# A paged-attention layer stack on one core: the first sample's loads spread over a tile, output weights in GpSimd's queue, one value block read by VectorE

## The chip, the cores and the metric

The kernel runs on one core of a Trainium2 chip. A core has five engines that run side by side: TensorE (matrix products, transposes), VectorE, ScalarE, GpSimd, and SyncE (SP), which here only issues DMAs. They meet through semaphores. The 16 DMA engines of the core serve SP's queue and GpSimd's queue. The metric is device time in microseconds of one execution, the median of several runs.

## The reference

64 samples of 32 tokens with 512 features go through four residual steps. The last is by far the heaviest:

```python
q, k, v = x @ Wq, x @ Wk, x @ Wv                 # 32 query heads, 8 key/value heads of 128
q, k = rope(rmsnorm(q)), rope(rmsnorm(k))
kc, vc = k_cache[block_table], v_cache[block_table]      # 16 pages of 32 positions per sample
scores = q @ concat([kc, k]) * SCALE             # masked to cache_seqlens
o = softmax(scores) @ concat([vc, v])
x = x + o @ Wo
```

Everything is float32 in the reference; the kernel splits numbers into a high and a low 16-bit part and multiplies the parts.

## The kernel before

The program has three blocks, one after another, with all engines meeting between them (a wait for `PEq L884` in the trace is the meeting at the end of the projections): `mixing` (the first three steps), `projections` and `attention`.

`projections` runs over NT = 16 tiles of 128 rows (four samples each). A tile is BLK = 12 blocks of 512 columns: 8 of queries, 2 of keys, 2 of values. TensorE makes a block in 12 matrix products; for queries and keys ScalarE sums squares, VectorE multiplies by the rotation tables, GpSimd adds, TensorE transposes the heads, ScalarE and VectorE keep the high and low halves, and SP stores them (`store_heads`). Each value block is read from PSUM twice by ScalarE (lines 1318, 1319), once in float32 and once in bfloat16; GpSimd forms the rest (`rest`), ScalarE the middle part (`middle`), GpSimd the lowest (`rest_low`), one tile later. Beside this the cache and output weights are split in chunks: SP loads chunk m + 2 and stores chunk m - 1 (`chunks`), ScalarE and VectorE split it. Once a tile ScalarE takes a square root (line 1293). SP's queue also carries the two DMA transposes of the next tile's input (`turn_x`, line 1088).

All SP work is one hand-written order: `body(t, p)` goes over the 12 blocks `n` and issues what is due. At the last block of tile EARLY = 12, `first_sample` (line 1096) waits for what it needs and calls `load_sample`, `load_fresh` and `load_row_scales`: everything of sample 0 that attention will need, 30 DMAs. Sample 1 is sent in pieces in the last tile (`second_sample`, line 1113).

`attention` has units of one sample and one key head: U = 32 units in a group of four samples, 512 in all. Per unit TensorE makes scores, transposes the probabilities of two units ago, and weighs values of three units ago; from the second group on it also projects one head of the group before (`project`). VectorE adds the mask and finds the maximum, ScalarE takes exponentials, VectorE normalises, GpSimd splits the probabilities of the new tokens (`new_tokens`, line 1735), which TensorE transposes (`turn_new`). There are two buffers for keys: SP fetches sample b when the scores and exponentials of sample b - 2 are done (`load`, line 1667): new keys, query, four small loads of scales (line 145), 16 pages (line 169), and four loads of fresh values (line 186). GpSimd gathers the values (line 1730). The output weights, 8 chunks of 1 MB, are issued by SP too: `WO_BEHIND` says behind which sample, four at the start and one behind each of samples 2 to 5, and `load_wo` waits for the chunk before (lines 1684 to 1688):

```python
if c:
    sp.wait_ge(wo_in[(c - 1) % 2], 16 * ((c - 1) // 2 + 1))
heads = (c * WOH, (c + 1) * WOH)
sp.dma_start(wo_of(*heads), wo_d[:, heads[0]:heads[1], :, :]).then_inc(wo_in[c % 2], 16)
```

TensorE waits for a chunk every fourth head of the first projected group (line 1833).

## Time and profile before

| | us |
|---|---|
| median of 3 runs (2137.56 to 2142.57) | 2138.86 |
| profiled execution | 2142.95 |
| its span | 2141.2 |
| TensorE busy | 2067.9 (97%) |
| VectorE busy | 1679.1 (78%) |
| ScalarE busy | 1476.0 (69%) |
| GpSimd busy | 1104.0 (52%) |
| DMA | 514.10 MB, 240 GB/s in the mean |

`mixing` ends and `projections` begins before 197 us, attention begins at 755.6 us. In the rows below, a timeline row gives the start and the duration in us, the engine, the line of the kernel, the operation with its output and inputs, and in brackets how long the engine had been idle before it and whom it waited for. PE is TensorE, PEld its weight loads, DVE VectorE, ACT ScalarE, POOL GpSimd, SPq the queue of SP. A window row gives for each engine the busy us and the instructions in a stretch, then the granted clock of TensorE as a share of full speed, the busy share of the DMA engines, and GB/s.

### The profile page before, as it was taken

The numbers are of one execution on the slowest core, as the hardware profiler recorded it, in microseconds if no ns is written. First come the engines' busy times: TensorE is split into PE (matmuls) and PEld (weight loads), VectorE is DVE, ScalarE is ACT, GpSimd is POOL, SyncE is SP. The second block draws the span as 40 slices with busy tenths as digits, with TensorE's granted clock in tenths as the row PEclk, the third lists the DMA queues.
The fourth block names the chain that finished last, engine by engine and source line by source line (L and its number), as shares of the span: only waits on it lengthen the run. The fifth ranks groups of instructions, "written<-read, shape, count | busy, mean of one in ns | idle before, by whom it ended". The sixth has DMA issues, their size and how long they took to land.

```text
span 2141.2 us, 55701 instructions
## 1 busy us (share of the span) xinstructions
PE 2067.9 (97%) x17214; PEld 1349.8 (63%) x17214; DVE 1679.1 (78%) x4282; ACT 1476.0 (69%) x4204; POOL 1104.0 (52%) x1855
## 2 busy tenths in 40 slices
PE   7989999999998978999999999999999999999999
PEld 3544555555554556777777777777777777777775
DVE  6897888888886676777777777777777777777774
ACT  2457777777776666777777777777777777777774
POOL 4456656565665634545454445455454545454542
PEclk9999999999999989999999999999999999999999
DMA  7755778776777778888888878788888888888881
GB/s 277 267 215 169 248 226 249 225 243 201 233 239 221 245 249 280 260 249 251 247 259 246 253 244 262 238 254 251 248 250 250 252 254 245 251 255 247 250 242 57
DMA packets 417577, 514.10 MB, mean 240 GB/s; under 512 B 67299, under 2 KB 313955, under 8 KB 416260
## 3 DMA queue, kind: packets, MB, share of 16 engines
q1 hardware_dynamic: 379828, 375.65, 57.5%
q0 software_dynamic: 37456, 134.89, 19.6%
q8 instruction: 142, 2.33, 0.4%
q14 instruction: 151, 1.24, 0.2%
HBM read 413.91 MB, written 92.54 MB: 237 GB/s over the span
## 4 chain that ended last, share of the span: by engine, by line
PE 60%; SPq 1%; DMA 1%; issue 1%; DVE 1%; ACT 0%; DVEq 0%; POOL 0%; POOLq 0%; ACTq 0%
PE att_y L1839 15%; PE att_scores L1789 15%; PE att_tr L1798 11%; PE att_o L1825 5%; PE att_o L1826 5%; PE att_o L1827 5%; PE att_tr_new L1804 1%; PE att_o L1828 1%; PE att_scores L1790 1%; DMA w<-wo_parts 1%; SPq L169 1%; DMA room<-k_parts 1%; SPq L145 0%; DVE att_prob L1942 0%; DVE att_tpl L1966 0%
## 5 line engine op out<-in xcount | busy, mean ns | idle before, releaser
L1942 DVE CUSTOM_DVE_ANT_0 att_prob<-att_scores,att_mask 128x544 f32<-128x544 f32 x512 | 370.9, 724 | 292.3 <-PE att_scores L1790 239.3
L1868 ACT ACTIVATE att_tph<-att_tr 128x512 f16<-128x512 f32 x512 | 305.9, 597 | 329.6 <-PE att_tr L1798 321.9
L1872 ACT ACTIVATE att_prob<-att_prob,att_col,rscale 128x544 f32<-128x544 f32 x512 | 430.7, 841 | 55.1 <-DVE att_col L1948 17.4
L1740 POOL CAST att_parts<-att_norm 128x96 f16<-128x96 f32 x512 | 135.1, 264 | 569.9 <-issue 556.8
L1966 DVE TENSOR_TENSOR att_tpl<-att_tr,att_tph 128x512 f16<-128x512 f32 x512 | 350.3, 684 | 1.1 <-ACT att_tph L1868 0.9
L1798 PE MATMUL att_tr<-ident,att_norm 128*128 128x128 f32 x2048 | 327.4, 283 | 0.0
L1354 POOL TENSOR_TENSOR proj_rn<-proj_ra,proj_rb 128x512 f32<-128x512 f32 x128 | 188.6, 1474 | 203.9 <-DVE proj_rb L1482 202.7
L1825 PE MATMUL att_o<-att_tph,w 128*128 128x128 f16 x1536 | 284.4, 219 | 2.8 <-ACT att_of L1868 2.4
L1826 PE MATMUL att_o<-att_tpl,w 128*128 128x128 f16 x1536 | 284.4, 219 | 0.0
L1827 PE MATMUL att_o<-att_tph,w 128*128 128x128 f16 x1536 | 284.4, 219 | 0.0
L1798 PEld LDWEIGHTS att_tr<-ident,att_norm 128*128 128x128 f32 x2048 | 216.5, 142 | 61.9 <-issue 1.4
L1959 DVE TENSOR_SCALAR att_norm<-att_prob,att_col 128x544 f32<-128x544 f32 x512 | 254.2, 497 | 1.0 <-issue 1.0
L1249 ACT ACTIVATE proj_square<-proj_blk 128x128 bf16<-128x128 f32 x640 | 168.4, 283 | 115.5 <-PE proj_blk L1209 115.5
L1789 PE MATMUL att_scores<-room 128*128 128x512 f16 x768 | 225.2, 383 | 15.0 <-DMA room<-k_parts 5.3
L1789 PE MATMUL att_scores<-w 128*128 128x512 f16 x768 | 220.6, 377 | 1.8 <-DMA w<-k_parts 1.4
L1730 POOL DMA_INDIRECT w<-v_parts,att_idx x186 | 184.1, 990 | 48.0 <-POOL att_idx L1728 24.6
L1825 PEld LDWEIGHTS att_o<-att_tph,w 128*128 128x128 f16 x1536 | 150.6, 98 | 30.3 <-issue 2.2
L1478 DVE TENSOR_TENSOR proj_ra<-proj_blk,proj_ta 128x512 f32<-128x512 f32 x160 | 110.0, 688 | 71.2 <-ACT proj_square L1249 69.4
L1839 PE MATMUL att_y<-w,att_ot 128*128 128x512 f16 x576 | 155.6, 379 | 0.0
L1839 PE MATMUL att_y<-w,ot 128*128 128x512 f16 x576 | 151.9, 379 | 0.0
L1827 PEld LDWEIGHTS att_o<-att_tph,w 128*128 128x128 f16 x1536 | 150.6, 98 | 0.0
L1826 PEld LDWEIGHTS att_o<-att_tpl,w 128*128 128x128 f16 x1536 | 150.6, 98 | 0.0
(234 smaller groups left out, 5423.7 us busy)
## 6 DMA issues: line engine op xcount, KB each, us to landing
room<-k_parts SPq DMA_DIRECT2D x512, 128.0 KB
w<-k_parts SPq DMA_DIRECT2D x512, 128.0 KB
q_parts<-ot SPq DMA_DIRECT2D x128, 256.0 KB, 3.8
v_new_parts<-ot SPq DMA_DIRECT2D x64, 256.0 KB
room<-q_parts SPq DMA_DIRECT2D x32, 512.0 KB
w<-q_parts SPq DMA_DIRECT2D x32, 512.0 KB
w<-in_w_t SPq DMA_DIRECT2D x12, 1024.0 KB, 7.7
room<-in_k_t SPq DMA_DIRECT2D x8, 1024.0 KB, 7.3
```

The source lines that it names most:

```text
L1354: g.tensor_tensor(out[:, :], ra[n % 2][:, :], rb[n % 2][:, :], ALU.add).then_inc(sum_done, 1)
L1789: mm(old, a, k, start=start, stop=stop)
L1798: last = nc.tensor.transpose(tr[q][:, c * P:(c + 1) * P], old[:, c * P:(c + 1) * P], ident[:, :])
L1825: mm(out, vh, th, start=(c == 0), stop=False)
L1826: mm(out, vh, tl, start=False, stop=False)
L1827: mm(out, vl, th, start=False, stop=False)
L1839: last = mm(y_ps[:, :], ot[p][:, a, h, :], wo_of(h, h + 1)[:, 0, w, :], start=(h == 0 and start), stop=(h == HQ - 1 and stop))
L1868: copy = lambda out, in_, **kw: nc.scalar.activation(out, in_, ACT.Copy, **kw)
L1872: nc.scalar.activation(prob[q][:, :], prob[q][:, :], ACT.Exp, bias=col[q][:, 1:2], scale=row_scale(i), accum_out=col[q][:, 2:3]).then_inc( ...
L1942: v.tensor_tensor_reduce(out=prob[q][:, :], in0=sc[q], in1=mask[bi % 2][:, at:at + LK], scale=1.0, scalar=-3.0e38, op0=ALU.add, op1=ALU.ma ...
L1959: v.tensor_scalar(out=norm[q][:, :], in0=prob[q][:, :], scalar1=col[q][:, 3:4], scalar2=TOP, op0=ALU.mult, op1=ALU.mult).then_inc(norm_don ...
L1966: v.tensor_tensor(tpl[q][:, :], tr[q][:, :], tph[q][:, 0:L], ALU.subtract).then_inc(tl_done, 1)
```

## The change

Four edits. The first sample's loads: at the end of tile 12 only the new keys and the query are issued; in tile 13 `first_rest(n)` issues two pages behind each of blocks 0 to 7, the fresh values behind block 8, and the row scales of samples 0 and 1 behind blocks 9 and 10. The end of the projections: VectorE reads the last value block of the last tile, ScalarE's copies are reordered around the normalising of the keys, and GpSimd finishes value block 0 before block 1. The output weights: GpSimd issues all eight chunks at the start of attention with no wait between them, on one semaphore. And TensorE waits once, ahead of the first projected head, for all eight.

```diff
@@ projections, sync
-                load_sample(nc, sp, 0, 0, 0, keys[0], query[0], rscale[0], page0, k_d, kn_d, q_d, rs_d, early)
-                load_fresh(sp, 0, fresh[0], vn_d, early)
-                load_row_scales(sp, 1, rscale[1], rs_d, early)
+                load_new_keys(sp, 0, keys[0], kn_d, early)
+                load_query(sp, 0, 0, query[0], q_d, early)
+
+            def first_rest(n):
+
+                half, at = divmod(n * 2, NPP // 2)
+                if at == 0 and half < 2:
+                    early_pages[:] = pages_of(nc, 0, half, page0)
+                if half < 2:
+                    for j in (at, at + 1):
+                        load_page(sp, half * (NPP // 2) + j, early_pages[j], keys[0], k_d, early)
+                if n == 8:
+                    load_fresh(sp, 0, fresh[0], vn_d, early)
+                if n in (9, 10):
+                    load_row_scales(sp, n - 9, rscale[n - 9], rs_d, early)
...
+                    if t == EARLY + 1:
+                        first_rest(n)
@@ projections, scalar
                     if t == NT - 1 and n == BLK - 1:
+                        middle(t, 0)
                         for j in range(KB):
                             normalise_keys(t, p, j)
+
+                        break
...
-            for j in range(KB):
-                heads_high(NT - 1, QB + j)
-                middle(NT - 1, j)
+            heads_high(NT - 1, QB)
+            middle(NT - 1, 1)
+            heads_high(NT - 1, QB + 1)
@@ projections, gpsimd
             for j in range(VB):
                 rest(NT - 1, j)
-            for j in range(VB):
                 rest_low(NT - 1, j)
@@ projections, vector
             tiles(dve, body)
+
+            dve.wait_ge(blk_done, NT * BLK)
+            dve.wait_ge(v_read, NT * VB - 1)
+            dve.wait_ge(v_out, (NT - 1) * 4 * 16)
+            dve.wait_ge(vlow, (NT - 1) * VB)
+            j, bank, scale = VB - 1, blk[(BLK - 1) % NB], col[(NT - 1) % 2][:, 6:7]
+            for to in (v32[j][:, :], vp[:, 0, j * D:(j + 1) * D]):
+                last = v.tensor_scalar(out=to, in0=bank[:, :], scalar1=scale, scalar2=None, op0=ALU.mult)
+            last.then_inc(v_read, 1)
@@ attention, sync
-            def load_wo(c):
-                if c:
-                    sp.wait_ge(wo_in[(c - 1) % 2], 16 * ((c - 1) // 2 + 1))
-                heads = (c * WOH, (c + 1) * WOH)
-                sp.dma_start(wo_of(*heads), wo_d[:, heads[0]:heads[1], :, :]).then_inc(wo_in[c % 2], 16)
...
-                    for c in WO_BEHIND.get(t * BT + bi, ()):
-                        load_wo(c)
@@ attention, gpsimd
+            def load_wo(c):
+                heads = (c * WOH, (c + 1) * WOH)
+                g.dma_start(wo_of(*heads), wo_d[:, heads[0]:heads[1], :, :]).then_inc(wo_in, 16)
...
+            for c in range(HQ // WOH):
+                load_wo(c)
             body(0, 0, 0)
@@ attention, tensor
-                if t == 0 and h % WOH == 0:
-                    pe.wait_ge(wo_in[h // WOH % 2], 16 * (h // WOH // 2 + 1))
+                if t == 0 and h == 0:
+                    pe.wait_ge(wo_in, 16 * (HQ // WOH))
```

## Rows read from the trace of the kernel before

**Rows 1.** Windows: us, busy us (instructions) of each engine, clock, DMA share, GB/s.
```profile
594.00:630.00 36.00, 34.88 (x182) 18.40 (x181) 29.87 (x54) 27.39 (x115) 23.43 (x20) 1.00 0.71 214
630.00:666.00 36.00, 28.40 (x134) 14.35 (x132) 20.99 (x38) 19.88 (x88) 15.54 (x11) 0.86 0.81 254
...
795.90:818.40 22.50, 18.55 (x192) 14.13 (x192) 16.71 (x50) 14.92 (x36) 11.29 (x24) 0.92 0.92 295
...
841.80:862.90 21.10, 21.07 (x190) 15.13 (x191) 14.00 (x42) 12.42 (x31) 6.76 (x18) 0.86 0.87 279
...
1005.00:1215.00 210.00, 209.46 (x2146) 151.39 (x2144) 165.50 (x489) 151.34 (x359) 105.33 (x229) 1.00 0.83 251
```

**Rows 2.** Timeline of SP's queue at the end of tile 12: start, duration, what.
```profile
630.24 0.56 SPq L150 DMA_DIRECT2D room<-k_new_parts  x1
...
636.13 9.09 SPq L169 DMA_DIRECT2D room<-k_parts  x16
...
647.14 1.81 SPq L145 DMA_DIRECT2D rscale<-q_row_scales  x4
```

**Rows 3.** Timeline of ScalarE: its square roots of three tiles, and a chunk.
```profile
233.89 0.24 ACT L1293 ACTIVATE proj_ss<-proj_ss 128x40 f32<-128x40 f32 x1 [2.69 <-DVE proj_ss L1442]
...
626.90 0.24 ACT L1293 ACTIVATE proj_ss<-proj_ss 128x40 f32<-128x40 f32 x1 [3.00 <-DVE proj_ss L1442]
...
652.39 0.72 ACT L1228 ACTIVATE proj_chunk_parts<-proj_chunk,up 128x512 f16<-128x512 f32 x1 [10.40 <-DMA proj_chunk<-in_wo_t]
...
674.19 0.24 ACT L1293 ACTIVATE proj_ss<-proj_ss 128x40 f32<-128x40 f32 x1 [3.00 <-DVE proj_ss L1442]
```

**Rows 4.** Timeline of TensorE in the projections, where it had been idle.
```profile
629.41 0.39 PE L1207 MATMUL proj_blk<-w,proj_xt 128*128 128x512 f16 x1 [1.12 <-DMA proj_xt<-xl]
...
654.47 1.09 PE L1186 MATMUL proj_tq<-ident,proj_rn 128*128 128x128 f32 x4 [7.60 <-DVE ot L1488]
```

**Rows 5.** Timeline of TensorE in attention's first 33 units, where it had been idle.
```profile
755.59 0.59 PE L1789 MATMUL att_scores<-room 128*128 128x512 f16 x1 [4.90 <-PEq L884]
...
795.97 0.39 PE L1789 MATMUL att_scores<-room 128*128 128x512 f16 x1 [0.71 <-DMA room<-k_parts]
805.60 0.23 PE L1825 MATMUL att_o<-att_tph,room 128*128 128x128 f16 x1 [1.82 <-DVE att_tpl L1966]
...
818.45 0.39 PE L1789 MATMUL att_scores<-w 128*128 128x512 f16 x1 [1.36 <-DMA w<-k_parts]
...
841.83 0.61 PE L1789 MATMUL att_scores<-room 128*128 128x512 f16 x1 [4.61 <-DMA room<-k_parts]
```

**Rows 6.** Timeline of SP's queue in attention: weights, scales of samples 3 and 6.
```profile
761.66 14.78 SPq L1688 DMA_DIRECT2D w<-wo_parts  x4
...
796.57 6.51 SPq L145 DMA_DIRECT2D rscale<-q_row_scales  x4
...
866.36 2.71 SPq L145 DMA_DIRECT2D rscale<-q_row_scales  x4
```

**Rows 7.** Timeline of ScalarE at the end of the projections: keys normalised.
```profile
747.53 2.44 ACT L1228 ACTIVATE xc<-xc,inv 128x128 f32<-128x128 f32 x8 [0.42 <-DVE inv L1464]
```

**Rows 8.** Timeline of VectorE at the same place.
```profile
747.47 0.69 DVE L1488 TENSOR_TENSOR ot<-proj_tq,ot 128x512 f16<-128x512 f32 x1
```

**Rows 9.** Timeline of GpSimd from the projections' end to attention's first split.
```profile
751.20 1.16 POOL L1359 TENSOR_TENSOR xc<-xc,ot 128x512 f32<-128x512 f32 x1 [3.90 <-ACT ot L1228]
752.31 2.26 POOL L1364 TENSOR_TENSOR ot<-xc,ot 128x512 bf16<-128x512 f32 x2
761.38 0.26 POOL L1740 CAST att_parts<-att_norm 128x96 f16<-128x96 f32 x1 [6.80 <-DVE att_norm L1959]
```

**Rows 10.** DMA queues from 766.6 to 771.3 us: packets, MB, share of 16 engines.
```profile
q1 hardware_dynamic: 144, 1.05, 64.7%
```

**Rows 11.** Instructions of GpSimd's DMA lines: count, min/median/max ns, first and last start.
```profile
L607 POOL DMA_DIRECT2D weights_most<-pow x1: 620/620/620, 70.5 to 70.5; - x1
...
L1730 POOL DMA_INDIRECT w<-v_parts,att_idx x186: 967/973/1086, 793.5 to 2093.2; - x186
```

More of the change, by code:

```diff
@@ L1106, in first_sample @@
                     sp.wait_ge(c_out[i], 16 * SPLIT)
-                load_sample(nc, sp, 0, 0, 0, keys[0], query[0], rscale[0], page0, k_d, kn_d, q_d, rs_d, early)
-                load_fresh(sp, 0, fresh[0], vn_d, early)
-                load_row_scales(sp, 1, rscale[1], rs_d, early)
-            second_pages = []
+                load_new_keys(sp, 0, keys[0], kn_d, early)
[11 more added lines that the diff above has]
+                    load_row_scales(sp, n - 9, rscale[n - 9], rs_d, early)
+            early_pages = []
             def second_sample(n):
@@ L1120, in second_sample @@
                 if at == 0 and half < 2:
-                    second_pages[:] = pages_of(nc, 1, half, page0)
+                    early_pages[:] = pages_of(nc, 1, half, page0)
                 if half < 2:
                     for j in (at, at + 1):
-                        load_page(sp, half * (NPP // 2) + j, second_pages[j], keys[1], k_d, early)
+                        load_page(sp, half * (NPP // 2) + j, early_pages[j], keys[1], k_d, early)
                 if n == 5:
@@ L1599, in attention @@
         y_ps = ctx.enter_context(nc.psum_tensor("att_y", [P, D], F32))
-        wo_in, unmasked = [sem(f"wo_in{i}") for i in range(2)], sem("unmasked")
+        wo_in, unmasked = sem("wo_in"), sem("unmasked")
         kq_in = [sem(f"keys_in{i}") for i in range(2)]
@@ L1631, in quad_views @@
             return src, [ot[p][:, a, heads, bi * S:(bi + 1) * S] for a in range(2)]
-        WO_BEHIND = {0: (0, 1, 2, 3), 2: (4,), 3: (5,), 4: (6,), 5: (7,)}
         def wo_of(first, last):
```

## The prediction

> **What bounds the kernel now.** I read the table of windows first. In the long steady part of attention TensorE is busy 209.46 of 210 us at the full granted clock, and the DMA engines are busy 0.83 of the time [rows 1]: there only TensorE's own work counts, and nothing in this change touches it. So a gain can come only from places where TensorE stands still or runs at a low granted clock. I then listed TensorE's idle times in order of time, and for each looked up the timeline of the engine that it waited for. Three places are near the edit. (1) Tile 13 of the projections: an idle time of 7.60 us [rows 4], and a granted clock of 0.86 in that window instead of 1.00 [rows 1]. (2) The change from projections to attention: 4.90 us idle [rows 5]. (3) The first 33 units of attention (a unit is one sample and one key head): idle times of 0.71, 1.82, 1.36 and 4.61 us [rows 5], with the clock at 0.92 and 0.86 in two windows [rows 1]. After unit 32 TensorE never waits for long, so what is won before it is won at the end.
>
> **Part A, the first sample page by page.** At the end of tile 12 SP issues the whole sample in one go, from 630.24 to 648.95 us [rows 2]: 18.7 us in which it issues nothing else. ScalarE needs the next chunk of raw weights and waits 10.40 us for it [rows 3]; its squares stop, VectorE stops, and TensorE stops for a free head buffer [rows 4]. The price is read best from ScalarE's square root, once a tile: 233.89 to 626.90 us is 11 tiles of 35.73 us; the tile with the stall takes 674.19 - 626.90 = 47.29 us [rows 3]. So 11.6 us are there to be won, idle time and low clock together.
>
> What the edit puts in its place: SP keeps all 30 issues, but in tile 13 has two pages behind each of eight blocks, 2 x 9.09/16 = 1.14 us each [rows 2], and one group of small loads, some 1.8 us, behind each of blocks 8, 9 and 10. A block takes 35.73/12 = 2.98 us. SP's queue also carries chunk loads and stores, head stores and the two transposes of the next tile's input. A chunk load is issued two chunks ahead of its use, three to four blocks or 9 to 12 us, and a quarter of a megabyte lands in less than the 4.9 us that 1 MB takes [rows 6], so a lag of a few us is covered. The transposes have no such cover: TensorE already waited 1.12 us for them at 629.41 [rows 4], and two pages are now ahead of them (1.1 us). The DMA engines are the second limit. A normal tile uses 0.71 x 36 = 25.6 us of them [rows 1]. A sample in steady attention uses 0.83 x 21 = 17.4 us (210 us are ten samples [rows 1]); less its value gathers of 2 MB, at 3.04 us per MB (64.7% of 4.7 us for 1.05 MB [rows 10]), that is 11.3 us. Tile 13 then needs 36.9 us of DMA in 36 us: full. Between ends of 0 and 6.6 us I take 2.0 for both effects, near the wait that the transposes already show. **A = 11.6 - 2.0 = 9.6 us** (5 to 11.6).
>
> **Part B, the last value block on VectorE.** Before, ScalarE normalises the keys from 747.53 to 749.97 [rows 7] and only then reads the second value block; GpSimd has waited 3.90 us for that and runs until 754.57 [rows 9]. TensorE's first score starts 1.02 us later [rows 5]. After: VectorE is free at 748.16 [rows 8], two reads of 0.69 us end at 749.5, GpSimd's first difference (1.16 us) at 750.7. ScalarE has one more copy ahead of the keys, so 747.53 + 0.6 + 2.44 + two copies gives 751.8; GpSimd's last difference (half of 2.26) ends at 752.9, VectorE's last low half about 753.1. VectorE takes the place of GpSimd as the last. **B = 754.57 - 753.1 = 1.5 us** (0.5 to 2.5).
>
> **Part C, output weights in GpSimd's queue.** Before, SP sends four chunks of 1 MB one after another, 14.78 us, and only at 776.44 begins sample 2; one further chunk stands ahead of each of samples 3, 4 and 5 [rows 6]. Behind a chunk the four small scale loads take 6.51 us, without one 2.71 [rows 6]: 3.8 us for each sample. TensorE's waits up to unit 32 are 0.71 + 1.82 + 1.36 + 4.61 = 8.5 us [rows 5]; the low clock costs 0.08 x 22.5 = 1.8 us and 0.14 x 21.1 = 3.0 us [rows 1]. That is 13.3 us at most.
>
> What takes their place: eight chunks without a wait are 8 x 3.04 = 24.3 us of DMA time, and six stores of 0.25 MB ahead of them 4.6 us, so from about 756 they are through at 785. The fetch of sample 2 waits for the exponentials of sample 0. Sixteen units took 795.26 - 755.59 = 39.7 us [rows 5], so eight take 19.8, and it begins near 754.1 + 19.8 = 774. It meets 11 us of chunks and has 11.3 of its own: 796.3. TensorE would be there at 795.26 - 1.5 = 793.8, so it waits 2.5 us (0.7 before), and I charge 1.8 us of low clock as in the window before. Samples 3 and 4 have no chunk ahead; 2 x 3.8 us saved is more than their 1.36 + 4.61 us of waits, and the 1.82 us behind value gathers go with the lighter traffic. TensorE needs the weights from unit 33 on, some 50 us after they have landed; that it now waits for all at once costs nothing.
>
> GpSimd is held while it issues. Its plain DMA took 0.62 us, its gathers 0.97 to 1.09 [rows 11]: 5.0 to 8.7 us for eight. It is first needed 5.8 us into attention [rows 5, 9], and TensorE another 1 us later. I take 0.62 plus 0.3 us between issues, 7.4 us, a loss of 0.7 (0 to 2). **C = 13.3 - 2.5 - 1.8 - 0.7 = 8.3 us** (3 to 13.3).
>
> A rule that speaks against the move: the 186 gathers that GpSimd issued beside VectorE's work are none of them longer than 1.09 us [rows 11]. The Trainium skill, SBUF — State Buffer, section "A bandwidth-pool intuition that's wrong (but worth ruling out)", says that a DMA of GpSimd which takes about 620 ns alone takes about 3100 ns beside a copy on VectorE, since its descriptors wait for a port that the two share. By it eight issues take 24.8 us and the gain falls to about 3 us, an estimate from the page's figure; the trace's gathers don't show it.
>
> **Sum.** 9.6 + 1.5 + 8.3 = 19.4 us. The profiled execution took 2142.95 us (span 2141.2) and would take 2123.5. It is 4.1 us above the median of the three runs, 2138.86; on the median's scale the forecast is **2119.5 us**.
>
> **Rivals.**
> *Tile 13 stays full.* The same issues and 36.9 us of DMA are in one tile; SP's lag eats the chunks' cover and A is about 4. For it: the share of 0.71 before anything is added. Against: SP's regular work in blocks 0 to 6 is one to three DMAs a block, so its lag is small until the transposes. 2138.86 - 4 - 1.5 - 8.3 = 2125. Chance 0.13.
> *The chunks starve sample 2.* Their rows are 8 KB, the pages' 1 KB; if the engines serve queues by turns, pages crawl until 785, and then need some 15 us for issue and landing (776.44 to 795.97 is 19.5 for the whole sample, small loads included). TensorE waits 6.2 us, not 2.5, at a low clock for longer: 2125. Chance 0.14. The Trainium skill, DMA: Bandwidth & Descriptors, "Issuing engines are not separate DMA queues", says that another queue saves issue time only.
> *VectorE delays GpSimd's issues.* Each waits for one VectorE operation, 0.62 + 0.69 us [rows 8, 11]: 10.5 us, 4 us past need, 2124. Chance 0.05. This is the skill's rule as rows price it.
> *The stall is only moved* (the change doesn't do what it says): ScalarE waits in pieces for head stores and chunks, and A is nothing: 2129. Chance 0.05.
> *GpSimd is held until each chunk has landed*, the one that ends slower. A chunk took 14.78/3 = 4.93 us [rows 6], eight 39.4 us; GpSimd's first split of the new tokens comes 33.6 us late, TensorE stands for it, and only the 2.5 us at sample 2 are saved: 19.4 - 31.1 = -11.7, so 2150.5. It decides from a hold of 5.8 + 19.4 + 2.5 = 27.7 us, 3.5 us per issue. Against: the gathers leave GpSimd after 1 us while they are still in flight. Chance 0.05.
>
> **How the numbers follow.** The forecast has 0.58; alone it spans 2115 to 2124. The bounds of A, B and C add up to gains of 8.5 and 27.4 us: 2111.5 to 2130.5, which takes in the first three rivals and the fourth; outside are the last one and sums of several, under 0.2. A measurement here tells about 0.2%, 4.3 us, from no change. The slower case gives 0.05; another 0.05, taken from the forecast and the middle rivals, is for several together, which would end within 4.3 us; faster is 0.90.
>
> **What would show it.** Right, A: the square roots around tile 13 lie about 37.7 us apart, and no chunk wait over 1 us. B: TensorE's first score 1.5 us nearer to its last transpose. C: GpSimd issues eight DMAs in under 9 us, its first split is at most 2 us late, SP's scale loads take under 3 us for samples 3 to 5, TensorE waits 2 to 3 us at unit 16 and hardly at 24 and 32. Wrong: a gap of GpSimd over 10 us, a wait of TensorE for the output weights at unit 33, an interval of tile 13 over 42 us, or new waits in steady attention.

## The result, and the profile after

| | before | after |
|---|---|---|
| median of 7 runs each | 2139.11 us | 2128.31 us |
| lowest and highest run | 2137.56 to 2142.57 | 2125.24 to 2132.66 |
| profiled execution, its span | 2142.95, 2141.2 | 2128.11, 2126.1 |

The ratio is 0.9945, with a 95% interval of 0.9932 to 0.9957: the change wins 11.8 us (9.2 to 14.5), and the medians are 10.8 us apart. The forecast was 2119.5, a gain of 19.4. The direction was right and the time lies in the range of 2111.5 to 2130.5, but outside the 2115 to 2124 to which the forecast itself had given most of its chance: about 0.6 of the forecast gain arrived.

Three landmarks divide both traces into the parts A, B and C of the prediction: ScalarE's square root once a tile, TensorE's first score of attention, and VectorE's first result of a tile of attention. First the roots of tiles 12 to 15 in the changed kernel, from ScalarE's timeline (start, duration, engine, line, operation, in brackets the idle time before it and what ended it), with one head copy that came late:

```profile
628.10 0.24 ACT L1307 ACTIVATE proj_ss<-proj_ss 128x40 f32<-128x40 f32 x1 [3.00 <-DVE proj_ss L1458]
...
663.84 0.24 ACT L1307 ACTIVATE proj_ss<-proj_ss 128x40 f32<-128x40 f32 x1 [1.25 <-DVE proj_ss L1458]
...
667.77 0.60 ACT L1242 ACTIVATE ot<-proj_tq 128x512 f16<-128x512 f32 x1 [1.91 <-DMA q_parts<-ot]
...
703.01 0.24 ACT L1307 ACTIVATE proj_ss<-proj_ss 128x40 f32<-128x40 f32 x1 [3.00 <-DVE proj_ss L1458]
...
737.12 0.24 ACT L1307 ACTIVATE proj_ss<-proj_ss 128x40 f32<-128x40 f32 x1 [1.02 <-DVE proj_ss L1458]
```

Tile 13 takes 663.84 - 628.10 = 35.74 us where it took 47.29 [rows 3]. The whole stall is gone, and tile 13 is a normal tile, not the 37.7 us of the forecast. But tile 14 takes 703.01 - 663.84 = 39.17 us, 3.7 more than the 35.44 that it took in the trace of before (709.63 - 674.19). The roots of tiles 14 and 15 there:

```profile
709.63 0.24 ACT L1293 ACTIVATE proj_ss<-proj_ss 128x40 f32<-128x40 f32 x1 [3.00 <-DVE proj_ss L1442]
743.83 0.24 ACT L1293 ACTIVATE proj_ss<-proj_ss 128x40 f32<-128x40 f32 x1 [1.02 <-DVE proj_ss L1442]
```

The same place in the changed kernel's timelines of TensorE and of SP's queue shows why:

```profile
668.77 0.39 PE L1221 MATMUL proj_blk<-w,xt 128*128 128x512 f16 x1 [2.42 <-DMA xt<-xl]
```
```profile
657.87 2.95 SPq L139 DMA_DIRECT2D v_new_parts<-ot  x4
661.00 1.27 SPq L169 DMA_DIRECT2D room<-k_parts  x2
662.31 0.49 SPq L1069 DMA_DIRECT2D wo_parts<-proj_chunk_parts  x1
662.85 0.43 SPq L1063 DMA_DIRECT2D proj_chunk<-in_wo_t  x1
663.38 0.45 SPq L1046 DMA_DIRECT2D q_parts<-ot  x1
663.94 1.30 SPq L1088 DMA_TRANSPOSE xt<-xh  x1
665.29 1.73 SPq L1088 DMA_TRANSPOSE xt<-xl  x1
```

SP falls behind at the end of tile 13: the transposes are issued only at 663.94 and 665.29, behind two pages, a chunk and stores. TensorE waits 2.42 us for the low half of the next input, where it waited 1.12 at the start of tile 13 in the kernel before [rows 4], and ScalarE 1.91 us for a head store that freed its buffer late. The windows (us, then busy us and instructions of PE, PEld, DVE, ACT and POOL, clock, DMA share, GB/s) show the new traffic of tile 13 and what follows:

```profile
631.00:667.00 36.00, 35.35 (x184) 18.52 (x182) 28.85 (x53) 26.34 (x112) 21.91 (x18) 1.00 0.95 311
667.00:703.00 36.00, 34.23 (x179) 18.29 (x180) 27.88 (x47) 25.09 (x109) 21.87 (x18) 1.00 0.71 212
...
1005.00:1215.00 210.00, 209.63 (x2149) 151.64 (x2147) 165.00 (x492) 151.84 (x359) 105.70 (x229) 1.00 0.83 251
```

The DMA share of tile 13 is 0.95, and the clock 1.00 where it was 0.86. Steady attention is the same to 0.2 us in 210 [rows 1], as assumed.

The change to attention, from the timelines of TensorE, VectorE and GpSimd:

```profile
747.05 0.58 PE L1811 MATMUL att_scores<-room 128*128 128x512 f16 x1 [2.24 <-PEq L884]
...
789.78 0.39 PE L1811 MATMUL att_scores<-room 128*128 128x512 f16 x1 [3.49 <-DMA room<-k_parts]
```
```profile
745.81 0.69 DVE L1504 TENSOR_TENSOR ot<-proj_tq,ot 128x512 f16<-128x512 f32 x1 [0.96 <-ACT ot L1242]
```
```profile
744.88 1.15 POOL L1381 TENSOR_TENSOR ot<-xc,ot 128x512 bf16<-128x512 f32 x1 [0.74 <-ACT ot L1242]
747.44 3.25 POOL L1763 DMA_DIRECT2D w<-wo_parts  x6 [1.41 <-POOLq L884]
750.64 1.09 POOL L1763 DMA_DIRECT2D att_wo<-wo_parts  x2
752.83 0.26 POOL L1756 CAST att_parts<-att_norm 128x96 f16<-128x96 f32 x1 [1.10 <-DVE att_norm L1981]
```

GpSimd ends its last difference at 746.03 and VectorE its last low half at 746.50, so VectorE is now the last, 0.55 us ahead of TensorE's first score. All eight chunks of output weights are issued in 4.34 us, and then GpSimd waits 1.10 us for VectorE: the issues delay nothing, and the first split comes 5.8 us after the first score, as before. Of TensorE's four waits in the first 33 units [rows 5] one is left, 3.49 us at unit 16; at 24 and 32 it goes on without a stop. SP's small scale loads take 2.51 and 2.10 us for samples 3 and 4, but 4.54 us for sample 2, whose fetch meets the chunks:

```profile
768.05 4.54 SPq L145 DMA_DIRECT2D rscale<-q_row_scales  x4
...
787.90 2.51 SPq L145 DMA_DIRECT2D rscale<-q_row_scales  x4
...
811.07 2.10 SPq L145 DMA_DIRECT2D rscale<-q_row_scales  x4
```

Last, attention's results in both kernels, from the groups of instructions that write the result tile (count, min/median/max ns, first and last start), after and then before:

```profile
L1993 DVE SCALAR_TENSOR_TENSOR att_res<-att_y,oscale,att_res x16: 741/744/752, 912.3 to 2122.9; 128x512 f32<-128x512 f32 x16
```
```profile
L1971 DVE SCALAR_TENSOR_TENSOR att_res<-att_y,oscale,att_res x16: 740/742/750, 928.5 to 2138.0; 128x512 f32<-128x512 f32 x16
```

From first to last result is 1210.6 and 1209.5 us: whatever is won is won before the first result, at 912.3.

**The accounts of this pair.** A, from tile 12's root to tile 15's: 116.93 before, 109.02 after, 7.9 won. B, from there to the first score: 11.76 and 9.93, 1.8 won. C, from the first score to the first result: 172.9 and 165.25, 7.7 won. Together 17.4; the start is 1.2 us later and the rest 1.1 longer, and the spans differ by 15.1. So in this one pair of traces B and C came close to their forecasts (1.5 and 8.3) and A fell 1.7 short, while the medians differ by 10.8. How much of 7.9, 1.8 and 7.7 is the change, and how much is this execution, had to be found with more traces.

### The profile page after: what moved, and what is told of

Same layout as the page of the kernel before. It is cut to its first block, busy times and chain, and to the rows that moved or that the text cites. A ratio compares the mean times of both kernels' runs of the same rounds, so it can differ in the third digit from the quotient of the medians.

```text
span 2126.1 us, 55700 instructions
## 1 busy us (share of the span) xinstructions
PE 2062.6 (97%) x17214; PEld 1348.2 (63%) x17214; DVE 1680.2 (79%) x4284; ACT 1477.9 (70%) x4202; POOL 1111.0 (52%) x1863
## 3 DMA queue, kind: packets, MB, share of 16 engines
q0 software_dynamic: 38608, 143.28, 20.8%
q14 instruction: 151, 1.24, 0.2%
## 4 chain that ended last, share of the span: by engine, by line
PE 61%; SPq 1%; DMA 1%; DVE 1%; issue 1%; ACT 0%; POOL 0%; DVEq 0%; ACTq 0%; POOLq 0%
PE att_scores L1811 16%; PE att_y L1861 15%; PE att_tr L1820 11%; PE att_o L1847 5%; PE att_o L1848 5%; PE att_o L1849 5%; PE att_tr_new L1826 1%; PE att_o L1850 1%; PE att_scores L1812 1%; SPq L169 1%; DVE att_prob L1964 0%; SPq L145 0%; DMA w<-v_parts,att_idx 0%; DMA room<-k_parts 0%; DMA w<-k_parts 0%
## 5 line engine op out<-in xcount | busy, mean ns | idle before, releaser
L1894 ACT ACTIVATE att_prob<-att_prob,att_col,rscale 128x544 f32<-128x544 f32 x512 | 431.4, 843 | 54.8 <-DVE att_col L1970 19.4
L1221 PE MATMUL proj_blk<-w,xt 128*128 128x512 f16 x384 | 146.1, 381 | 6.4 <-PEq L311 3.9
```

Source lines behind the costliest of these rows:

```text
L1894: nc.scalar.activation(prob[q][:, :], prob[q][:, :], ACT.Exp, bias=col[q][:, 1:2], scale=row_scale(i), accum_out=col[q][:, 2:3]).then_inc( ...
```

## The experiments

**Theory.** The three parts act alone and add up. A gives about 7 because the lag of SP's queue reaches the transposes and stores of tile 14. C gives less than its sum since the eight chunks meet the fetch of sample 2. **Rivals:** the parts take from one another; tile 14 is late because the DMA engines are full; the wait at unit 16 comes from the new queue or its issue and not from the chunks' bytes.

Gains below are (1 - ratio) x the median of the kernel before that was measured beside the run (2141.42 us for e1 to e4, 2142.86 for e5 to e8, 2140.24 for e9 to e11), in brackets the 95% interval.

### One part alone, and all three again

e1 takes the kernel before and spreads the pages of the first sample (part A):

```diff
-                load_sample(nc, sp, 0, 0, 0, keys[0], query[0], rscale[0], page0, k_d, kn_d, q_d, rs_d, early)
-                load_fresh(sp, 0, fresh[0], vn_d, early)
-                load_row_scales(sp, 1, rscale[1], rs_d, early)
+                load_new_keys(sp, 0, keys[0], kn_d, early)
+                load_query(sp, 0, 0, query[0], q_d, early)
...
+                    if t == EARLY + 1:
+                        first_rest(n)
```

> The kernel before with the first sample's loads spread over tile 13, nothing else. Theory 1 (the parts add up as the two traces show): the interval of the square roots around tile 13 falls from 47.3 us to 36 to 37, the next one grows from 35.4 to about 39, and the time falls by 7.9 us. Theory 2 (the traced execution of the kernel before was about 4 us slower than its median because one of its stalls was longer than usual, and the part that stall belongs to is worth less in the median): if it is this one, the time falls by 4 us or less. Rival of the forecast (the stall is only moved): within 1 us of no change.

Measured: 2134.11 us, ratio 0.997, a gain of 6.4 (4.3 to 8.6). The two places of TensorE's timeline that bear on it, tile 14's start and then units 16, 24 and 32:

```profile
666.42 0.39 PE L1221 MATMUL proj_blk<-w,xt 128*128 128x512 f16 x1 [2.29 <-DMA xt<-xl]
...
788.82 0.39 PE L1803 MATMUL att_scores<-room 128*128 128x512 f16 x1 [0.44 <-DMA room<-k_parts]
...
811.05 0.61 PE L1803 MATMUL att_scores<-w 128*128 128x512 f16 x1 [3.31 <-DMA w<-k_parts]
...
832.97 0.39 PE L1803 MATMUL att_scores<-room 128*128 128x512 f16 x1 [1.95 <-DMA room<-k_parts]
```

Tile 13 took 35.86 us and tile 14 40.11. The gain lies between the two theories (7.9 and 4 or less), and its interval leaves out the 9.6 of the forecast. The wait for the transposed input is there without parts B and C, so it belongs to A.

e2 has part B alone:

```diff
                     if t == NT - 1 and n == BLK - 1:
+                        middle(t, 0)
                         for j in range(KB):
                             normalise_keys(t, p, j)
+
+                        break
...
+            for to in (v32[j][:, :], vp[:, 0, j * D:(j + 1) * D]):
+                last = v.tensor_scalar(out=to, in0=bank[:, :], scalar1=scale, scalar2=None, op0=ALU.mult)
+            last.then_inc(v_read, 1)
```

> The kernel before with the last value block read by VectorE and the end of the projections reordered, nothing else. Theory 1: from the last square root to the first score of attention 9.9 us instead of 11.8, and 1.8 us off the time. Theory 2 (what attention begins earlier is given back, since the fetch of samples 2 to 4 sets when units 16 to 32 run): 0 to 0.5 us off the time, with the same 9.9 us in the trace and a longer wait of TensorE for sample 2.

Measured: 2137.41 us, ratio 0.9982, a gain of 3.9 (1.7 to 6.2). In its trace the first score starts 751.57 - 741.73 = 9.84 us after the last root; before, this took 11.76. The sign of theory 2 is there too, a longer wait for sample 2 at unit 16:

```profile
795.05 0.61 PE L1800 MATMUL att_scores<-room 128*128 128x512 f16 x1 [4.70 <-DMA room<-k_parts]
```

But units 24 and 32 then wait for no keys, and the stretch from the first score to the first result is 169.7 us, not longer than the 172.9 of before. So this trace shows no loss of what B wins. It does show that a wait of this size at unit 16 can occur with the chunks in SP's queue.

e3 has part C alone:

```diff
-                    for c in WO_BEHIND.get(t * BT + bi, ()):
-                        load_wo(c)
...
+            for c in range(HQ // WOH):
+                load_wo(c)
             body(0, 0, 0)
```

> The kernel before with all eight chunks of output weights in GpSimd's queue at attention's begin and one wait of TensorE for all, nothing else. Theory 1: from the first score to the first result 165 us instead of 173, no wait at units 24 and 32, one of about 3.5 us at unit 16, and 7.7 us off the time. Theory 2 (the 4.6 us wait at unit 32 with its low clock was the unusual one in the trace of before): 3 to 5 us off the time. Rival (GpSimd held until chunks land): slower by 10 us or more.

Measured: 2136.09 us, ratio 0.9978, a gain of 4.7 (2.6 to 6.6), in the 3 to 5 of theory 2. The interval leaves out the 7.7 of theory 1 and the 8.3 of the forecast. TensorE waits at unit 16 alone, in this trace for less than the 3.5 us expected:

```profile
798.27 0.61 PE L1786 MATMUL att_scores<-room 128*128 128x512 f16 x1 [2.01 <-DMA room<-k_parts]
```

e4 is the changed kernel once more, measured beside its parts.

> The changed kernel once more, beside its three parts. Theory 1: the sum of the three parts, about 17 us below the kernel before. Theory 2: about 11 us below, and one of the three alone well below its share of the traces (7.9, 1.8, 7.7). A second trace of it shows which of its waits vary from execution to execution: at unit 16 (3.5 us in the first) and at tile 14's start (2.4 us).

Measured: 2128.36 us, ratio 0.9937, a gain of 13.5 (10.5 to 16.7), between the 11 and 17 of the two theories. The parts alone give 6.4 + 3.9 + 4.7 = 15.0. The parts add up within their intervals; a small give and take between them is not excluded. That rival falls, and the shortfall has to be looked for inside the parts.

### The kernel before, twice more

No edit: e10 and e11 are profiles of the kernel before, to see how much its own stretches vary.

> The kernel before once more, for its trace. Question: whether the 172.9 us from the first score to the first result, from which part C was worked out, were a usual execution. With the same attention code the pages-alone and the value-block-alone kernels took 169.9 and 169.7 us. Theory 1 (an unusual execution): 169 to 171 us, and waits of TensorE for pages of samples 2 to 4 that sum to 5 to 6 us instead of 6.7, with less low clock. Theory 2 (it is the time at which attention begins that makes the difference): 172 to 174 us again.

> The same once more, as one trace alone can't tell the two theories apart: theory 1 169 to 171 us, theory 2 172 to 174 us.

Measured: 2143.46 and 2139.47 us, one run each. From the first score to the first result e10 takes 173.6 us, which is theory 2's range, and e11 166.2, below the ranges of both. So neither theory is borne out: 172.9 is no rarity, and attention began at nearly the same time in all three (755.6, 755.1 and 757.8 us). What is shown is a spread of 7 us in one stretch of one program. Units 16, 24 and 32 of e10 and then of e11, from TensorE's timelines:

```profile
794.98 0.39 PE L1789 MATMUL att_scores<-room 128*128 128x512 f16 x1 [0.57 <-DMA room<-k_parts]
...
817.25 0.39 PE L1789 MATMUL att_scores<-w 128*128 128x512 f16 x1 [1.15 <-DMA w<-k_parts]
...
843.24 0.61 PE L1789 MATMUL att_scores<-room 128*128 128x512 f16 x1 [7.38 <-DMA room<-k_parts]
```
```profile
797.25 0.39 PE L1789 MATMUL att_scores<-room 128*128 128x512 f16 x1 [0.16 <-DMA room<-k_parts]
...
818.88 0.61 PE L1789 MATMUL att_scores<-w 128*128 128x512 f16 x1 [2.25 <-DMA w<-k_parts]
...
840.21 0.39 PE L1789 MATMUL att_scores<-room 128*128 128x512 f16 x1 [1.58 <-DMA room<-k_parts]
```

The same program waits 7.38 us at unit 32 in one execution and 1.58 in the other; 4.61 stood in [rows 5]. So the landmarks of all traces of one kind are put together:

| stretch | without the part | with the part | won |
|---|---|---|---|
| A, root 12 to root 15 | 116.93, e2 115.03, e3 116.88, e10 117.21, e11 116.71; mean 116.55 | after 109.02, e1 110.10, e4 110.35, e7 109.21, e8 108.61; mean 109.46 | 7.1 |
| B, root 15 to first score | 11.76, e1 11.94, e3 11.76, e10 11.75, e11 12.28; mean 11.90 | after 9.93, e2 9.84, e4 10.66, e5 11.37, e6 9.95, e7 9.80, e8 10.57, e9 12.13; mean 10.53 | 1.4 |
| C, first score to first result | 172.9, e1 169.9, e2 169.7, e10 173.6, e11 166.2; mean 170.5 | after 165.25, e3 164.3, e4 165.2, e5 167.65, e6 165.5; mean 165.6 | 4.9 |

(Each line holds the traces whose kernel leaves that stretch as it is before or after; e5 to e9 come next.) The sum is 13.4 us, against 13.5 and 11.8 by timing. The part of C that a single pair of traces makes 7.7 is 4.9 in the mean; 2.4 of the difference is that the profile of before lies above the mean there, 172.9 against 170.5. That mean is loose: five values from 166.2 to 173.6 put it within about 1.3 us (an estimate, their spread over the root of five), and of the three traces of the unchanged kernel two lie at 173. The 4.7 us by timing agree with it. B's 1.4 is smaller than the spread of B with the part, 9.80 to 12.13.

### Why tile 14 is late: order or bytes

e5 keeps tile 13's pages but puts none behind blocks 6 and 7, where the transposes are issued. They end two blocks later:

```diff
-                half, at = divmod(n * 2, NPP // 2)
...
+                step = n if n < 6 else n - 2
+                half, at = divmod(step * 2, NPP // 2)
+                if n not in (6, 7) and half < 2:
...
-                if n == 8:
+                if n == 10:
                     load_fresh(sp, 0, fresh[0], vn_d, early)
-                if n in (9, 10):
-                    load_row_scales(sp, n - 9, rscale[n - 9], rs_d, early)
+                if n in (10, 11):
+                    load_row_scales(sp, n - 10, rscale[n - 10], rs_d, early)
```

> The changed kernel with no page issued behind blocks 6 and 7 of tile 13; those four go behind blocks 8 and 9, after the two transposes, and the small loads one block later. The same DMAs in the same tile. Question: why is tile 14 of the projections 3.7 to 5.1 us longer than a normal one after the change, beginning with a wait of 2.1 to 2.4 us for the transposed input. Theory 1 (the order of SP's queue: pages stand ahead of the transposes): the wait falls to 1.1 us or less, as in tile 13, and the next interval of the square roots from 39-40.5 to 36-37. Theory 2 (the DMA engines are full in that tile, 0.95 to 1.0): the wait stays near 2 us and the interval above 38. By the time, theory 1 is 2 to 4 us faster than the changed kernel, theory 2 within 1 us of it.

Measured: 2126.33 us, ratio 0.9927, a gain of 15.6 (10.5 to 20.8); its interval overlaps with e4's, so timing alone can't rank the two. Its trace can. TensorE at tile 14's start, then SP's queue, then the window of tile 13:

```profile
667.27 0.39 PE L1222 MATMUL proj_blk<-w,xt 128*128 128x512 f16 x1 [0.63 <-DMA xt<-xl]
```
```profile
662.80 1.31 SPq L1088 DMA_TRANSPOSE xt<-xh  x1
664.15 1.41 SPq L1088 DMA_TRANSPOSE xt<-xl  x1
```
```profile
631.00:667.00 36.00, 35.62 (x184) 18.68 (x184) 29.03 (x53) 27.40 (x115) 22.11 (x19) 1.00 0.97 304
```

The DMA share is 0.97, as full as before the edit, and yet the wait falls to 0.63 us and stretch A to 106.75, below all five with two pages behind every block (108.61 to 110.35). The two timelines say where the wait went. The issue of the low half begins 1.45 us after the root in the changed kernel (665.29 - 663.84) and 0.27 us before it in e5 (664.15 - 664.42). From the end of that issue to TensorE's start it is 1.75 us in the one (668.77 - 667.02) and 1.71 in the other (667.27 - 665.56): the transfer is no quicker, it is issued sooner. So the order of SP's queue costs most of it, 109.46 - 106.75 = 2.7 us, by this one trace against the mean of five. Some 1.6 us stay: tile 14 took 37.08 us. The full DMA engines may have a share in these, since SP's own issues were longer in that tile: its four value stores took 2.95 us in the changed kernel and 2.65 in e5, and 2.00 in the same tile of the kernel before, at 665.02; that share isn't parted.

e6 gives the first sample two tiles, one page behind a block instead of two:

```diff
-            def first_rest(n):
+            def first_rest(t, n):
...
-                if half < 2:
-                    for j in (at, at + 1):
-                        load_page(sp, half * (NPP // 2) + j, early_pages[j], keys[0], k_d, early)
-                if n == 8:
+                if n < 8:
+                    if n == 0:
+                        early_pages[:] = pages_of(nc, 0, t - EARLY - 1, page0)
+                    load_page(sp, (t - EARLY - 1) * (NPP // 2) + n, early_pages[n], keys[0], k_d, early)
+                if t == EARLY + 2 and n == 8:
...
-                    if t == EARLY + 1:
-                        first_rest(n)
+                    if t in (EARLY + 1, EARLY + 2):
+                        first_rest(t, n)
```

> The changed kernel with one page behind each of blocks 0 to 7 of tiles 13 and 14, and the small loads in tile 14: half the DMA load per tile, and half the pages ahead of the transposes. Both theories on tile 14's wait expect it at 1.1 us or less in both tiles and intervals of 36 to 37 us, so 3 to 4 us faster than the changed kernel (some 16 us below the kernel before). If it does no better than the changed kernel, neither the order nor the load of the DMA engines is the cause.

Measured: 2125.7 us, ratio 0.9933, a gain of 14.4 (9.6 to 19.3). At tile 14's start TensorE no longer waits for its input, and the tiles 13 and 14 take 36.76 and 35.45 us; A is 106.06. Tile 13 and tile 14 in its windows:

```profile
631.00:667.00 36.00, 35.18 (x183) 18.71 (x184) 29.01 (x51) 26.20 (x113) 22.55 (x19) 1.00 0.91 300
667.00:703.00 36.00, 35.89 (x187) 18.77 (x184) 30.32 (x56) 27.52 (x115) 21.84 (x18) 1.00 0.72 226
```

TensorE is busy 71.07 of these 72 us, against 69.58 in the changed kernel. It is the better place for the pages, by the trace; the timing agrees but doesn't tell it from e4 either.

### What the wait at unit 16 is

e7 sends six chunks at attention's begin and holds back two, until GpSimd has reached steps 9 and 17 of its second body. Their heads have a semaphore of their own:

```diff
+                    if past == 1 and i in (9, 17):
+                        load_wo(6 if i == 9 else 7)
...
-            for c in range(HQ // WOH):
+            for c in range(6):
                 load_wo(c)
...
-                    pe.wait_ge(wo_in, 16 * (HQ // WOH))
+                    pe.wait_ge(wo_in[0], 16 * 6)
+                if t == 0 and h == 6 * WOH:
+                    pe.wait_ge(wo_in[1], 16 * 2)
```

> The changed kernel with six chunks of output weights at attention's begin, and the last two issued by GpSimd in units 41 and 49, with waits of TensorE at heads 0 and 24. Question: what is the wait of 3.5 to 4.2 us at unit 16, with the low clock after it. Theory 1 (the chunks share the DMA engines with sample 2; two chunks less are 6.1 us of DMA time): the wait falls to 1 us or less, from the first score to the first result takes 161 to 162 us instead of 165, 3 to 4 us faster than the changed kernel. Theory 2 (SP's own issue time of sample 2 sets it, 18 to 19 us whatever else runs): the wait stays at 3 us or more and the time within 1 us of the changed kernel.

Measured: 2122.59 us, ratio 0.992, a gain of 17.1 (11.1 to 23.1). No wait for keys is left in the first 33 units, and C is 160.5 us. The two late chunks leave GpSimd one by one after the crowded stretch:

```profile
849.77 0.58 POOL L1763 DMA_DIRECT2D att_wo<-wo_parts  x1
...
870.80 0.58 POOL L1763 DMA_DIRECT2D att_wo<-wo_parts  x1
```

e8 is the floor: it loads one chunk only. It leaves out seven of the eight chunks and projects all heads with the weights of the first four.

```diff
-            for c in range(HQ // WOH):
-                load_wo(c)
+            load_wo(0)
...
-                    pe.wait_ge(wo_in, 16 * (HQ // WOH))
+                    pe.wait_ge(wo_in, 16)
...
-                    last = mm(y_ps[:, :], ot[p][:, a, h, :], wo_of(h, h + 1)[:, 0, w, :], start=(h == 0 and start),
+                    last = mm(y_ps[:, :], ot[p][:, a, h, :], wo_of(h % WOH, h % WOH + 1)[:, 0, w, :], start=(h == 0 and start),
```

> The changed kernel with only the first of the eight chunks loaded; every head is projected with the weights of the first four heads, so the output is not the reference's. It gives the limit of what placing the weights can win: no wait at unit 16 if theory 1 of the chunks holds, and from the first score to the first result about 160 us; under theory 2 (SP's own issue time) the wait at unit 16 stays and it takes 164 or more.

Measured: 2124.17 us in a single run, with C at 160.0 us and no wait for keys. So with one chunk left in front of sample 2 that stretch takes 160.0; e7 with all its chunks reaches that to 0.5 us. The bytes of the chunks in front of sample 2 are the cause of the wait, not the issue on GpSimd, which e7 keeps for six of them: the five traces with all eight chunks there wait 2.0 to 4.4 us for keys at unit 16 (after, e3 to e6), the three with six or one (e7, e8 and e9) not at all. The window of sample 2's fetch, in the changed kernel and in e7:

```profile
766.90:789.80 22.90, 17.13 (x193) 12.74 (x192) 17.58 (x52) 15.53 (x39) 11.84 (x24) 1.00 0.91 305
```
```profile
767.00:789.80 22.80, 20.25 (x228) 15.25 (x227) 20.25 (x61) 17.56 (x43) 12.18 (x26) 1.00 0.76 234
```

With two chunks fewer the DMA share falls from 0.91 to 0.76, and TensorE does 228 matmuls in that window, not 193. How the chunks delay the fetch can be seen from 767 to 770 us, just after SP issued its first load of sample 2 (767.19 in the changed kernel, 767.10 in e7). The DMA queues (packets, MB, share of 16 engines; q0 is GpSimd's, q1 SP's), the changed kernel and then e7:

```profile
q0 software_dynamic: 172, 1.28, 100.9%
```
```profile
q0 software_dynamic: 61, 0.37, 29.4%
q1 hardware_dynamic: 332, 0.23, 23.7%
```

In the changed kernel GpSimd's queue has the engines alone for these 3 us: SP's queue moves no packet. SP then needs 4.54 us for the four small scale loads (2.32 in e7) and reaches the first page 6.35 us after the fetch began (773.54 - 767.19), against 4.62 us (771.72 - 767.10). The sixteen pages themselves take it 10.11 and 9.94 us.

### Both repairs together

e9 has e6's two tiles and e7's six and two chunks, the edits as shown above.

> The changed kernel with both repairs: pages one per block over tiles 13 and 14, and six chunks at attention's begin with two later. If the two causes are what the single runs show, the traces add up: 35.5 to 37 us between the square roots in both tiles (106 us for the three tiles instead of 109 to 110), 160 to 161 us from the first score to the first result instead of 165, and 2119 to 2121 us in all, some 20 us below the kernel before. If the wait at unit 16 comes back because attention begins earlier, it is 165 us again and 2124.

Measured: 2120.09 us (2119.52 to 2122.58), ratio 0.9906, a gain of 20.1 (16.1 to 24.4). It has the lowest median of the kernels here, 8 us below the changed kernel, though its interval still overlaps with those of e4 and e7. Its stretches: A 106.02 (10.5 won), B 12.13 (0.2 lost), C 160.9 (9.6 won), 19.9 in sum. B is back at its old length in this trace; ScalarE waits there for stores:

```profile
737.61 0.69 ACT L1240 ACTIVATE xc<-proj_blk,xcol 128x512 f32<-128x512 f32 x1 [2.64 <-DMA v_new_parts<-ot]
...
740.01 0.60 ACT L1240 ACTIVATE ot<-proj_tq 128x512 f16<-128x512 f32 x1 [1.14 <-DMA q_parts<-ot]
```

Neither edit touches SP's queue in the last tile, and e6 and e7 alone have 9.95 and 9.80 us there. But e5 too has such waits of ScalarE for head stores (1.79 and 1.24 us) and a B of 11.37, with another edit. So this may be variation between executions; no second trace of e9 was taken.

## Why the prediction was right or wrong

**What bounds the kernel: right.** Steady attention didn't move, and all the gain lies before the first result of attention, as the landmarks show.

**A, forecast 9.6, measured 7.1 (6.4 by timing).** The 11.6 us to be won were won in full in this pair of traces: tile 13 went from 47.29 to 35.74 us (11.2 in the means). The term that was mis-sized is the 2.0 for what takes their place: 11.6 - 7.1 = 4.5. Tile 14 alone took 2.7 to 5.1 us more than 35.44 in the five traces. I had read the row of the transposes rightly as the place without cover, but priced it by the wait that stood there already (1.12 us). Two pages ahead of the transposes come on top of an old lag, and the wait became 2.42 (2.15 to 3.00 in the five traces), with 1.91 us behind a head store. In e1 and e4 the granted clock fell after it, to 0.70 and 0.79 from 665 to 670 us; that cost the forecast didn't have at all. I also looked for the loss in tile 13, while it falls into tile 14; the sign named in the prediction (roots 37.7 us apart) misses it. Of the cause I had put SP's lag and full DMA engines into one term. e5 parts off 2.7 us for the order; the 1.6 us that stay in it are open. The rival *tile 13 stays full* fails in its words, since tile 13 ran at a share of 0.95 with TensorE busy 35.35 of 36 us (0.97 and 35.62 in e5), although its A of 4 was in the right direction and SP's lag was real: it fell on the transposes and not on the chunks. *The stall is only moved* fails: 3.7 of 11.6 us came back in the next tile.

**B, forecast 1.5, measured 1.4 by the stretches, 3.9 by timing.** The steps came as written: VectorE took GpSimd's place as the last, by 0.47 us. The interval of the timing begins at 1.7, just above both. e2's own stretch A was 1.5 us shorter than the mean without a reason in the edit, but that is one execution and the 3.9 rests on eleven. What else e2 wins, if anything, stays open.

**C, forecast 8.3, measured 4.9 (4.7 by timing).** Here the mechanism was right: issue under 9 us (4.34), scale loads under 3 us for samples 3 to 5 (2.51, 2.10 and 2.10), nothing at units 24 and 32, a wait at unit 16. Two sizes were off. First, the 13.3 us of waits and low clock to be won came from one execution. Its stretch was 172.9 us, the mean of five is 170.5 and the floor is 160.0 (e8, one trace), so 10.5 were there to be won, 2.8 fewer. For that one execution the 13.3 was nearly right: 172.9 - 160.0 = 12.9. Second, the charge of 2.5 + 1.8 + 0.7 = 5.0 was 165.6 - 160.0 = 5.6. The wait itself was mis-sized: 3.49, 2.01, 4.20, 4.37 and 3.82 us in five traces, mean 3.6, not 2.5; GpSimd's 0.7 was nothing. So of C's miss of 3.4 us by the means 2.8 is the base and 0.6 the charges, with the looseness of the means said above. The step that failed is one of method: I read the base from one execution and then moved the *whole* sum to the median's scale by one subtraction of 4.1 us, as if the excess of that execution lay outside of the stretches I was pricing. By the means 2.4 us of it lay inside C. The 4.1 itself rests on three runs; against 2141.42, the median of 27 runs beside e1 to e4, the excess is 1.5.

**The other rivals.** *The chunks starve sample 2* asked for 6.2 us at unit 16; the mean is 3.6, so its size is half true. Its mechanism is nearer to the trace than the fair sharing that I took: SP's queue moved nothing from 767 to 770 us. But it was the small loads that stood and not the pages, and the chunks were through earlier than forecast: GpSimd's queue was done with them at about 774 us, 27 us after the first score, where the forecast had 785 - 754.1 = 31. The Trainium skill, DMA: Bandwidth & Descriptors, "Issuing engines are not separate DMA queues", says that another queue saves issue time only. The trace agrees: SP is free of the chunks, but unit 16 waits 3.49 us, with the same engines serving both queues, where it waited 0.71. *VectorE delays GpSimd's issues* and *GpSimd is held until each chunk has landed* both fail: 4.34 us for eight issues, 0.54 us each, while VectorE ran its mask and first maximum, and the chunks landed 13.8 to 23.1 us (medians of the two groups) after their issue.

**The sum.** 19.4 forecast; 9.6 + 1.5 + 8.3 became 7.1 + 1.4 + 4.9 = 13.4. The measured gain is 11.8, and 13.5 beside the parts. The range held it since the bounds of A (5) and C (3) were wide enough for two misses in one direction. That the time lies in it is luck more than merit: the time is 4 us above the band of the main case, and no rival gives it for the reason found. That e9 then wins 20.1 (16.1 to 24.4) shows that the forecast size was there to be had, but not with this placement of pages and chunks.

## What to carry to other kernels

When loads are spread between the issues of a queue, list what the queue issues at its most crowded step, and charge the lag to the item there with no cover (here two transposes), in the tile where it is consumed and not in the tile of the load. Before a sum is built on waits for a nearly full DMA, take two or three traces of the unchanged kernel: the same waits were 1.58 and 7.38 us. Moving bytes to an idle queue relieves the old queue's issue order, but bytes that stand in front of an urgent fetch still delay it: here two of eight chunks, not needed for some 50 us, were better held back until it had passed.

## What the runs showed of the hardware

- Nearly full DMA engines alone didn't stop TensorE: with a share of 0.97 in tile 13 it was busy 35.62 of 36 us (e5).
- Two queues didn't share the DMA engines evenly: with chunks of 1 MB in GpSimd's queue, SP's queue moved no packet from 767 to 770 us, though its loads had been issued from 767.19 on (changed kernel).
- GpSimd issued eight plain DMAs of 1 MB in 4.34 us, with none waiting for an earlier one to land. The Trainium skill, SBUF — State Buffer, "A bandwidth-pool intuition that's wrong (but worth ruling out)", has 3100 ns for a DMA of GpSimd beside a copy on VectorE; by that figure eight would take 24.8 us, an estimate. Here each took 0.54 us. VectorE ran a memset, a mask and a maximum beside them, no plain copy, so the runs don't test the page's own case.
- The clock after a short stop isn't the same from run to run. In the changed kernel TensorE stood 2.42 us at tile 14's start, and in e7 3.00 us, and the granted clock stayed at 1.00 from 665 to 675 us in both; in e1 it stood 2.29 us and 665 to 670 us had 0.70, so it ran for a part of it at the lower level, 1.2 GHz:

```profile
665.00:670.00 5.00, 3.58 (x10) 1.37 (x11) 2.10 (x4) 2.91 (x7) 0.00 (x0) 0.70 0.51 137
```
